# Fused cross-attention and six-layer local-attention/FFN kernel: norm scratch moved from PSUM to SBUF, one semaphore per dependency, and new slot orders on all engines

## What is computed

```python
for i in range(6):
    x = attn_layer(shift_tokens(x), Wqkv[i], q_scale[i], k_scale[i], Wo[i]) + x
    x = ffn_layer(shift_tokens(x), ln_g[i], ln_b[i], W1[i], b1[i], W2[i], b2[i]) + x
# attn_layer: q, k, v of 16 heads x 64; q and k divided by their l2 norm per head,
# scaled, rotated by position; softmax in windows of 32 queries over the same and
# the previous 32 keys; then @ Wo
# ffn_layer: xn = (x - mean) / sqrt(var + 1e-5) * g + b
#            a, gate = split(xn @ W1 + b1);  (a * gelu(gate)) @ W2 + b2
# shift_tokens: the upper 64 channels of each token come from the token before
```

## Time and profile before

| what | value |
|---|---|
| time, median of 3 runs (lowest, highest) | 3308.8 us (3306.87, 3309.24) |
| span of the profiled execution, first to last instruction | 3304.7 us |
| PE busy (matmul) | 3125.4 us, 95% |
| DVE busy | 2884.0 us, 87% |
| ACT busy | 2663.4 us, 81% |
| POOL busy | 2447.9 us, 74% |
| mean granted TensorE clock | 0.978 of 2.4 GHz |
| DMA queues, share of 16 engines' span | 21.2% (181.55 MB) |

### The profile page before, as it was taken

One profiled execution on the slowest core, in us unless ns is written; L12 is line 12 of the kernel. 1 busy time (PEld: TensorE's weight loads), 2 busy tenths in 40 slices (PEclk: granted clock), 3 DMA queues, 4 the chain that ended last, 5 costly groups with the idle time before them and its releaser, 6 DMA issues.

```text
span 3304.7 us, 181505 instructions
## 1 busy us (share of the span) xinstructions
PE 3125.4 (95%) x71268; PEld 2192.5 (66%) x71268; DVE 2884.0 (87%) x6045; ACT 2663.4 (81%) x5440; POOL 2447.9 (74%) x2673
## 2 busy tenths in 40 slices
PE   6776899999999999999999999999999999999996
PEld 4443567676667676676767667676676767667665
DVE  7886789999899999899999899998899999899984
ACT  6886678888788888788888788888788888788874
POOL 3333778888788888788888778787787878788883
PEclk9988999999999999999999999999999999999997
DMA  3000112122222222222222212122221212212121
GB/s 79 8 7 10 47 51 59 50 59 71 67 56 53 56 53 77 63 54 55 54 55 74 68 50 59 50 59 77 57 59 50 59 50 77 66 50 59 50 58 50
DMA packets 150374, 182.24 MB, mean 55 GB/s; under 512 B 51572, under 2 KB 74162, under 8 KB 149554
## 3 DMA queue, kind: packets, MB, share of 16 engines
q1 hardware_dynamic: 150322, 181.55, 21.2%
HBM read 21.32 MB, written 2.10 MB: 7 GB/s over the span
## 4 chain that ended last, share of the span: by engine, by line
PE 57%; issue 13%; DVE 10%; ACT 10%; POOL 5%; SPq 1%; DVEq 1%; DMA 1%; ACTq 1%; POOLq 0%
PE bank L1252 13%; PE bank L1339 8%; PE bank L1322 7%; PE bank L1262 5%; PE bank L1363 5%; PE bank L1270 3%; PE bank L1290 3%; ACT L798 3%; DVE tb L966 3%; ACT P L774 3%; PE bank L1392 2%; ACT gl L766 2%; POOL qk L524 2%; DVE bank L1075 2%; PE bank L1400 2%
## 5 line engine op out<-in xcount | busy, mean ns | idle before, releaser
L533 POOL TENSOR_TENSOR qk<-qk,rn 128x512 f32<-128x512 f32 x768 | 803.0, 1046 | 356.8 <-DVE rn L985 356.8
L524 POOL TENSOR_TENSOR qk<-ta,tb 128x512 f32<-128x512 f32 x768 | 978.6, 1274 | 2.5 <-DVE tb L966 2.5
L1252 PE MATMUL bank<-wqkv,zsT 128*128 128x512 f32 x1536 | 819.9, 617 | 25.4 <-ACT vt L705 12.3
L963 DVE TENSOR_TENSOR ta<-bank,rot 128x512 f32<-128x512 f32 x768 | 527.5, 687 | 116.1 <-ACT sq L688 87.4
L966 DVE TENSOR_TENSOR tb<-bank,rot 128x512 f32<-128x512 f32 x768 | 523.0, 681 | 0.0
L1068 DVE TENSOR_REDUCE bank<-sq 128x32 f32<-128x2048 f32 x192 | 440.6, 2295 | 25.1
L688 ACT ACTIVATE sq<-bank 128x512 f32<-128x512 f32 x768 | 445.2, 611 | 14.8 <-PE bank L1252 12.1
L696 ACT ACTIVATE qkT<-bank 128x512 f32<-128x512 f32 x768 | 396.6, 602 | 57.1 <-PE bank L1290 56.9
L1363 PEld LDWEIGHTS bank<-wo,oT 128*128 128x128 f32 x3072 | 375.4, 193 | 92.4 <-issue 92.4
L743 ACT ACTIVATE znT<-bank,small 128x128 f32<-128x128 f32 x192 | 87.9, 458 | 431.8 <-PE bank L1383 431.8
L564 POOL TENSOR_TENSOR P<-P,rowsum 128x512 f32<-128x512 f32 x384 | 392.9, 1045 | 20.0 <-DVE rowsum L1083 20.0
(11 more groups left out here) (131 smaller groups left out, 5740.6 us busy)
## 6 DMA issues: line engine op xcount, KB each, us to landing
vs<-vt SPq DMA_DIRECT2D x1152, 128.0 KB, 2.4
wqkv<-L_ffn_Wqkv SPq DMA_DIRECT2D x6, 1024.0 KB, 5.0
zm<-zm SPq DMA_DIRECT2D x192, 31.8 KB
wqkv<-L_ffn_Wqkv SPq DMA_DIRECT2D x6, 512.0 KB, 3.7
wo<-L_ffn_Wo SPq DMA_DIRECT2D x6, 512.0 KB, 4.0
z_sb<-x SPq DMA_DIRECT2D x4, 512.0 KB, 5.1
ctxb<-ctx SPq DMA_DIRECT2D x32, 64.0 KB, 1.8
w<-L_ffn_W SPq DMA_DIRECT2D x6, 341.0 KB
```

The lines of the kernel that those rows point to most:

```text
L524: g.tensor_tensor(o, i0, i1, ALU.add).then_inc(s["g_add"], 1)
L533: g.tensor_tensor(q3, q3, r3, ALU.mult).then_inc(s["g_qk"], 1)
L963: v_.tensor_tensor(ta[:, c].rearrange("p (h d) -> p h d", d=DH), bank[j % 2][:, :].rearrange("p (h d) -> p h d", d=DH), rot[:, o:o + 64].u ...
L1252: t_.matmul(bank[j % 2][:, :], zsT[:, pu, :], wqkv[:, 512 * j:512 * j + 512], start=True, stop=True).then_inc(s["p_qk"], 1)
```

## The change

What it does:

1. The norm scratch (sums of squares sm, n0, n1) and the softmax row sums rs get SBUF tiles of their own. `root(0)`, a tensor_scalar maximum, becomes a scalar_tensor_tensor with sm as both inputs; `root(2)`, a tensor_tensor product, becomes a scalar_tensor_tensor with a factor 1.0. The Newton step's four instructions now read two SBUF operands; before, one of their tensors was in PSUM.
2. The second norm (zn) is a scalar_tensor_tensor: mean as the scalar, rstd broadcast along the row as second tensor, in place of a tensor_scalar with two per-partition scalars.
3. Each dependency has its own semaphore that goes up by one for each unit (p_qk0 to p_qk3, d_rot0 to d_rot3, ...). Waits through `edge` are only issued outside the loop, where the unit is a plain number; in the loop an engine relies on the other waits and the order. One pair of slots in the loop holds, besides its real work, this many register and sequencer instructions: PE 34 before, 14 after; DVE 37 and 19; ACT 38 and 13; POOL 28 and 15.
4. New slot orders on PE, ACT, DVE and POOL. PE's list is now zT(n+1), qk2(n), PT(n-3), S(n-2), qk3(n), znT(n-4), AV(n-3), gate(n-4), v0(n), a(n-4), v1(n), y(n-3), qk0(n+1), tr(n-1), y2(n-4), qk1(n+1).
5. SyncE's list keeps its order; its waits take the new names. An additional constant tile (eps) is filled and not used.

The diff, cut to its core (POOL, ACT and PE only have their steps reordered and their waits renamed):

```diff
+        sm = sb("sm", [128, 2 * HEADS])
+        n0 = sb("n0", [128, 2 * HEADS])
+        n1 = sb("n1", [128, 2 * HEADS])
+        eps = sb("eps", [128, 1])
+        rs = sb("rs", [128, HEADS])
...
+        def done(unit, total=UNITS):
+
+            return min(max(unit + 1, 0), total) if isinstance(unit, int) else unit + 1
+
+        def unit(n, k, lag, total=UNITS):
+
+            u = n - lag
+            return u, (not isinstance(u, int)) or 0 <= u < total, (k - lag) % 2
...
         def slots(eng, body, xbody):
-            body(-2, -2)
+            for n in range(-3, -1):
+                body(n, n)
...
             def load_qk(layer):
                 w = Wqkv[layer, :, :]
-                wait(sp, "p_qk", 4 * B * layer)
+                for j in range(4):
+                    wait(sp, f"p_qk{j}", B * layer)
...
+                u, on, p = unit(n, k, 4)
+                if on:
+                    wait(dve, "g_rstd", done(u))
+                    edge(dve, u, "p_znT", done(u - 1))
+                    v_.scalar_tensor_tensor(zn[:, :], zm[:, p, 0:2, :].rearrange("p c e -> p (c e)"), mv[:, 0:1],
+                                           rstd[:, p:p + 1].to_broadcast([128, E]), ALU.subtract, ALU.mult).then_inc(s["d_zn"], 1)
+
+                u, on, p = unit(n, k, 1)
+                if on:
+                    edge(dve, u, "d_nr1", done(u))
+                    v_.scalar_tensor_tensor(n1[:, :], n0[:, :], 1.0, rn[:, p, :], ALU.mult, ALU.mult).then_inc(s["d_nr2"], 1)
...
+                    v_.scalar_tensor_tensor(rn[:, p, :], n1[:, :], 1.5, rn[:, p, :], ALU.add, ALU.mult).then_inc(s["d_rn"], 1)
...
+                    v_.tensor_reduce(sm[:, :], sq[:, :].rearrange("p (h d) -> p h d", d=DH), AX.X, ALU.add).then_inc(s["d_sumsq"], 1)
...
+                    v_.scalar_tensor_tensor(sm[:, :], sm[:, :], NORM_MIN2, sm[:, :], ALU.max, ALU.max).then_inc(s["d_nr0"], 1)
...
+                    v_.tensor_reduce(rs[:, :], P[:, p, :].rearrange("p (h t) -> p h t", t=DH), AX.X, ALU.add).then_inc(s["d_sum"], 1)
...
+                    v_.reciprocal(rowsum[:, :], rs[:, :]).then_inc(s["d_rec"], 1)
...
+                    v_.scalar_tensor_tensor(n0[:, :], sm[:, :], -0.5 * LN_UP, rn[:, p, :], ALU.mult, ALU.mult).then_inc(s["d_nr1"], 1)
```

More of the change, by code:

```diff
@@ L328, in load_w1 @@
                 wait(sp, "p_a", B * layer)
+                wait(sp, "p_gate", B * layer)
                 sp.dma_start(w1[:, :], W1[layer, :, :]).then_inc(s["l_w1"], 16)
@@ L343, in shift_v @@
             def shift_v(u, par):
-                for r in range(2):
-                    wait(sp, "a_v", count(2, u, r + 1))
+                for r in (0, 1):
+                    wait(sp, f"a_v{r}", done(u))
                     wait(sp, "p_AV", count(2, u - 2, 2))
@@ L783, in slot @@
[L783 to L799 removed]
+                u, on, p = unit(n, k, 0)
@@ new lines, in slot @@
+                u, on, p = unit(n, k, 4)
+                if on:
+                    wait(act, "p_gate", done(u))
+                    edge(act, u, "d_h", done(u - 1))
+                    for j, (_, m) in enumerate(FCH):
+                        ins = a_.activation(gl[0:m, j, :], bank[7][0:m, 128 * j:128 * j + 128], ACT.Gelu, bias=small[0:m, 5 + j:6 + j])
+                    ins.then_inc(s["a_gelu"], 1)
+                u, on, p = unit(n, k, 4)
+                if on:
+                    act.preload_act_table_set("natural_log_exp_and_others")
@@ L1108, in slot @@
+                u, on, p = unit(n, k, 3)
+                if on:
+                    wait(dve, "d_agg", done(u))
+                    v_.tensor_scalar(ve[:, p:p + 1], mv[:, 1:2], LN_EPS, None, ALU.add).then_inc(s["d_ve"], 1)
                 if isinstance(n, int) and UNITS <= n < UNITS + 4:
@@ new lines, in slot @@
+                u, on, p = unit(n, k, 4)
+                if on:
+                    wait(pe, "a_zn", done(u))
+                    edge(pe, u, "a_zs", done(u + 5))
+                    wait(pe, "l_w1", 16 * layer_of(u) + 16)
+                    for j, (o, m_) in enumerate(FCH):
+                        ins = t_.matmul(bank[7][0:m_, 128 * j:128 * j + 128], w1[:, FF + o:FF + o + m_], znT[:, :], start=True, stop=True)
+                    ins.then_inc(s["p_gate"], 1)
+                u, on, p = unit(n, k, 0)
@@ new lines, in slot @@
+                if on:
+                    edge(pe, u, "a_zs", done(u))
+                    edge(pe, u, "d_rot2", done(u))
+                    wait(pe, "l_wv", 16 * layer_of(u) + 16)
+                    t_.matmul(bank[0][:, :], zsT[:, p, :], wv[:, :, 0, :], start=True, stop=True).then_inc(s["p_v0"], 1)
+                u, on, p = unit(n, k, 4)
+                if on:
+                    edge(pe, u, "a_zn", done(u))
+                    wait(pe, "l_w1", 16 * layer_of(u) + 16)
+                    for j, (o, m_) in enumerate(FCH):
+                        ins = t_.matmul(bank[6][0:m_, 128 * j:128 * j + 128], w1[:, o:o + m_], znT[:, :], start=True, stop=True)
+                    ins.then_inc(s["p_a"], 1)
@@ new lines, in slot @@
+                u, on, p = unit(n, k, -1)
+                if on:
+                    wait(pe, "a_v0", done(u - 1))
+                    edge(pe, u, "a_zs", done(u))
+                    if isinstance(u, int) and u == 0:
+                        pe.wait_ge(s["x_add"], 4 * B)
+                    wait(pe, "l_wqk", 16 * layer_of(u) + 16)
+                    t_.matmul(bank[0][:, :], zsT[:, p, :], wqkv[:, 0:512], start=True, stop=True).then_inc(s["p_qk0"], 1)
+                u, on, p = unit(n, k, 1)
```

899 lines of the change are left out of this document (440 added, 459 removed), and 6 rows, old and new, of the table names.

## The result

The changed kernel takes 3204.3 us (median of four runs, 3201.4 to 3206.1) where the kernel before takes 3308.1 (3306.9 to 3309.2). The ratio is 0.969, with a 95% interval of 0.967 to 0.970: 3.1% faster. The prediction was 3235 us, 2.2% faster, with a range of 3190 to 3312. So sign and range held, and the size was 31 us short. The profiled execution after has a span of 3204.3 us, 100.4 less than the 3304.7 before.

A forecast was written before the change was run, and what follows sets the result against it. PE was to bound the loop at 14.70 us per slot instead of 15.03: 62 us over 187 slots plus 12 at layer changes, 74 off the 3304.7 span, 3231, plus 4.1 to the median: 3235 us, range 3190 to 3312.

The forecast's parts named there:

- The sum: Whole loop: all rings end between 13.9 and 14.6 us, PE bounds, with 0.1 added: 14.70 us per slot.
- The floor of 14.60: PE's list without any wait, taken from the old order's chain: 15.00 - 0.13 - 0.27 = 14.60 us per slot.
- the 0.1 that I added for handovers: Per slot, 0.1 us added to PE's 14.60 because so many handovers between engines are close.
- The lower end of 14.47: PE's slot if gate's extra 0.13 us, its weights waiting for ACT's copy, is covered by AV.
- rival 1: PE fully fed: gate's 0.13 us covered, nothing waits, 14.47 us per slot, 3192 us; chance 0.15.
- zn: Second norm on DVE: the new form takes 0.26 us in sequence, saving 0.27; bounds 0.26 and 1.06.
- POOL's holds: DVE instructions with two SBUF inputs beside POOL: sm's maximum 0.5 us, zn 0.2, n1 and rn nothing, n0 covered.
- DVE's ring: zm, shift, statistics and the rest of DVE's list: 13.9 us per slot free of POOL, 14.6 with 0.7 of holding.
- Rival 4: DVE held by POOL at sm's maximum and zn: ring 15.4 us per slot, slower at 3366 us; chance 0.14.
- Semaphores: Fewer register instructions in the loop: costed at nothing; +0.13 us per slot if the new order needs issue time again.
- Changes of layer: Statistics waiting for a shift queued behind weights: 2.5 us gained at each of five, 12 us; bounds 0 and 25.
- The signs: Expected in the profile: slots of 14.6 to 14.8 us, chain almost wholly PE, no Exp wait, zn 0.3 to 0.5 us.

The follow-up runs named there:

- the last run: Changed kernel without the maximum of sm, AV directly behind S, znT ahead of qk3, its copy ahead of AV's copies: 3214.6 us, ratio 0.972.

## Why the prediction was right, and where it was off

- **What bounds it.** Right: PE, fully fed. The sum took 14.70 us per slot and the loop shows 14.654: (15.033 - 14.654) x 187 = 71 us for 62. Two errors partly cancel in this. The floor of 14.60 was read off the old order; the new order's list has one block of small tiles more (three: PT with S, AV, and the q/k transposes; before, AV stood behind S) and takes 14.65 with nothing waiting. And the 0.1 that I added for handovers was not needed. The agreement of the slot to 0.05 us is thus in part luck.
- **Gate's weight load.** The lower end of 14.47, and rival 1, had gate's extra 0.13 us go once AV covers ACT's copy of znT. The copy is covered now: gate's weight load begins at AV's end with no wait. But gate then stands behind AV's small tiles, and costs 0.77 all the same; behind v0 and with the copy in time, in the last run, it costs 0.66. One cause went and another took its place. In the sum: the prediction's 14.47 and about 0.19 us for the third block of small tiles, by an estimate from the starts above, are the 14.65.
- **zn.** The amount was right (0.26 us in sequence, 0.34 as its row), the reason was wrong. I gave the saving to the new form, by the gated product's price; the old form takes as long in the new place, and the new one 0.67 in the old place. I also read rows 5 as two SBUF inputs at work, but zn's old form, which took 1.06 there, has a single tensor input beside two per-partition scalars. I had both rows before me, 0.346 us alone and 1.06 beside POOL, and should have priced the place.
- **POOL's holds.** sm's maximum was taken at 0.5 and measures 0.58 (0.76 less 0.18). n0 was to be held under the shift's cover: held for 0.8, and the statistics wait 27.9 us in the whole program. n1 and rn free: 0.18 each. The Trainium skill's rule ("SBUF — State Buffer", section "Who interferes with whom") agrees with the rows of these two: the maximum and n0, each with two SBUF inputs, are held to the end of POOL's instruction, and the maximum with one input, as a tensor_reduce, is not. That none of it costs time follows from which engine is the bound.
- **DVE's ring.** It was put at 13.9 free of POOL and 14.6 with 0.7 of POOL's holds (0.5 for the maximum, 0.2 for zn). The run with a shorter y gives DVE's list as 14.46. Close, but the prediction's picture of two rings at exactly 14.6 was too tight: DVE has 0.19 us of room.
- **Rival 4,** DVE held until it passes PE, had the mechanism right and the price wrong: it needed a ring of 15.4, and the holds came to 14.46.
- **Semaphores.** Priced at nothing. In the loop that is right for the waits (0.006 us per slot for all of them); the register instructions were not priced apart.
- **Changes of layer.** 2.5 us each, 12 in all, against 3.3 each and 16.5. What of the new order shortens them wasn't looked into.
- **The ends** carry most of the 31 us that were missing. They were priced at nothing, and gave 100.4 - 71 - 16.5 = 13 us: the first statistics comes 8.2 us earlier, and the last five slots, where each unit waits for its own shift, took 82.6 us and take 73.7. Why both got shorter is open. Of the span, the slots were 9 us short, layer changes 4.5, ends 13: 26.5; the remaining 4 us or so are the 4.1 that the prediction added from span to median. After, span and median are both 3204.3, because the profiled execution is the slowest of its four (3206.1 us): chance, not a gain.
- **The signs.** The chain of waits was to be almost wholly PE, and it was mostly DVE. With both engines busy over 99% of the time it named the engine that was not the bound. The statistics were to wait 0.3 to 0.8 us per slot for the shift; in the loop they don't wait, since n0's hold covers it. The other signs came as written: slots of 14.65, no wait for Exp, zn at 0.34.

## What to carry to other kernels

When two engines are both near 100% busy, neither busy time nor the chain of waits says which one sets the pace: take a known amount of work off each, and see which one the slot follows, and down to what. Price a held instruction by its place beside the other engine's work and not by its form alone, and then ask whether its engine is the bound at all. And when an order is rewritten, price the passages between tile shapes again, and count the ends and the phase changes: here three tenths of the gain lay outside the regular slots.

## What was not expected of the hardware

- Tile shapes on PE. A 512-column projection took 0.86 us ahead of full tiles and 0.95 or 0.96 ahead of tiles of 32 or 64 rows. Six 128-column matmuls took 0.66 behind full tiles and 0.77 behind small ones. In this kernel that is some 0.2 us per passage there and back, three times in a slot of 14.65.
- A 32-column maximum with two SBUF inputs (the same tensor twice) took 0.76 us at the median where a tensor_reduce with one input took 0.17, in the same place of the same order.
- Ten to twenty more wait instructions per slot on PE, DVE and ACT each, all long met, lengthened the slot by 0.006 us.
